# Splitting the experts' weights on Pool in layer 1 instead of layer 0 (a two-layer cross-attention and feed-forward kernel)

## The reference

```python
x = x + _L0_xattn_ref(_layernorm(x), ctx_768, ...)
x = x + _L0_ffn_ref(_layernorm(x), ...)        # int8-like fake quantisation, silu(gate) * up
x = x + _L1_xattn_ref(_layernorm(x), ctx_768, mask, ...)
x = x + _L1_ffn_ref(_layernorm(x), ...)        # 8 experts, all computed:

h = gelu(einsum('nd,edh->neh', xf, w1) + b1)   # w1: 8 x 128 x 256
y = einsum('neh,ehd->ned', h, w2) + b2         # w2: 8 x 256 x 128
out = (y * norm_g[:, None, None]).sum(axis=1)
```

## Time and profile before

| | us |
|---|---|
| median of 3 runs | 293.55 (293.08 to 295.0) |
| the profiled execution, its own time | 294.46 |
| the profiled execution, its span | 292.7 |
| PE busy | 265.0 (91%) |
| DVE busy | 205.5 (70%) |
| ACT busy | 203.7 (70%) |
| POOL busy | 101.6 (35%) |

### The profile page before, as it was taken

How to read it: one execution, slowest core, us unless ns; L and a number is a source line. 1 busy time by engine, 2 the same in 40 slices (tenths; PEclk the granted TensorE clock), 3 DMA queues, 4 the chain that set the end, 5 groups by cost and what they waited for, 6 DMA issues and landing times.

```text
span 292.7 us, 5757 instructions
## 1 busy us (share of the span) xinstructions
PE 265.0 (91%) x2075; PEld 189.3 (65%) x2075; DVE 205.5 (70%) x535; ACT 203.7 (70%) x303; POOL 101.6 (35%) x119
## 2 busy tenths in 40 slices
PE   8898989899998528888899999999999999999993
PEld 8776454655676217755545677776678578788872
DVE  3898776945996896799945886692548457745764
ACT  4735766188529837312677967898999996957991
POOL 3791996068950500120111000460202702107180
PEclk9999999999999995899999999999999999999999
DMA  7537000000000000000000000000000000000001
GB/s 232 164 85 212 1 2 3 0 2 0 2 1 2 0 0 0 2 0 1 2 3 2 0 2 0 2 0 3 0 36 3 0 0 2 0 37 2 0 1 72
DMA packets 4573, 6.45 MB, mean 22 GB/s; under 512 B 1181, under 2 KB 2898, under 8 KB 4546
## 3 DMA queue, kind: packets, MB, share of 16 engines
q1 hardware_dynamic: 3426, 3.47, 3.8%
q0 software_dynamic: 848, 2.35, 2.8%
q10 hardware_dynamic: 272, 0.27, 0.3%
HBM read 5.04 MB, written 1.05 MB: 21 GB/s over the span
## 4 chain that ended last, share of the span: by engine, by line
PE 53%; DVE 5%; ACT 2%; issue 2%; POOL 1%; DVEq 0%; POOLq 0%
PE ps L1107 6%; PE ps L1096 6%; PE ps L1109 5%; PE ps L1097 5%; PE ps L1098 5%; PE ps L1108 5%; PE ps L1006 3%; PE ps L988 2%; PE ps L947 2%; PE ps L968 1%; PE ps L1014 1%; PE ps L1042 1%; PE ps L1085 1%; DVE mxr L697 1%; ACT p L501 1%
## 5 line engine op out<-in xcount | busy, mean ns | idle before, releaser
L779 DVE TENSOR_TENSOR hhl<-hf,hhl 128x512 fp32r<-128x512 f32 x64 | 42.7, 689 | 26.7 <-ACT hf L571 24.0
L501 ACT ACTIVATE p<-ps 117x1024 f32<-117x1024 f32 (+1 forms) x48 | 46.2, 1021 | 15.1 <-PE ps L998 15.0
L697 DVE TENSOR_REDUCE mxr<-ps 128x8 f32<-128x616 f32 x64 | 47.6, 793 | 12.2 <-PE ps L978 12.0
L570 ACT ACTIVATE hhl<-ps,b 128x512 fp32r<-128x512 f32 x64 | 45.9, 717 | 10.4 <-PE ps L1109 6.0
L571 ACT ACTIVATE hf<-ps,b 128x512 f32<-128x512 f32 x64 | 46.0, 718 | 0.0
L888 PE MATMUL ps<-ones 128*128 128x128 f32 x230 | 36.8, 308 | 1.5 <-POOL ones L387 1.0
L888 PEld LDWEIGHTS ps<-ones 128*128 128x128 f32 x230 | 33.5, 219 | 6.5 <-issue 2.9
L344 POOL TENSOR_SCALAR veps<-mv 128x4 f32<-128x4 f32 x16 | 5.2, 327 | 81.8 <-DVE mv L627 81.6
L444 POOL TENSOR_TENSOR lq<-ebase,lg 128x32 f32<-128x32 f32 x4 | 22.3, 5587 | 19.0 <-DVE lg L818 18.9
L1107 PE MATMUL ps<-hhl,w2l 128*128 128x512 f32 x64 | 26.8, 419 | 0.0
L1096 PE MATMUL ps<-x1buf,w1l 128*128 128x512 f32 x64 | 26.4, 413 | 0.0
(11 more groups left out here) (188 smaller groups left out, 565.5 us busy)
## 6 DMA issues: line engine op xcount, KB each, us to landing
x<-in_x SPq DMA_DIRECT2D x4, 256.0 KB, 4.5
w1raw<-in_w POOLq DMA_DIRECT2D x1, 1024.0 KB, 6.3
w2raw<-in_w POOLq DMA_DIRECT2D x1, 1024.0 KB, 7.2
out<-xn SPq DMA_DIRECT2D x4, 256.0 KB, 2.1
ctxw<-in_ctxw SPq DMA_DIRECT2D x1, 280.0 KB, 5.1
kmo<-in_kmo POOLq DMA_DIRECT2D x1, 220.0 KB, 8.0
ctxw<-in_ctxw ACTq DMA_DIRECT2D x1, 192.5 KB, 3.5
wqo<-in_wqo SPq DMA_DIRECT2D x1, 192.0 KB, 5.6
```

The source lines that it names most:

```text
L501: act.activation(p[0:w, j, 2 * half:2 * half + 2, :], pair_of("key", u, j, half)[0:w], ACT.Exp, scale=SCALE).then_inc(q["p_ready"], 1)
L570: act.activation(hh[:, b % HR, :], bank_of("w1", 1, b), ACT.Gelu, bias=b1[:, b % NH:b % NH + 1])
L697: nc.vector.tensor_reduce(mxr[:, u % 2, j, 2 * half:2 * half + 2, :], heads[:, :, :, 0:M], AX.X, ALU.max).then_inc(q["tok_maxed"], 1)
L779: nc.vector.tensor_tensor(hl[:, b % HR, :], hf[:, b % HF, :], hh[:, b % HR, :].bitcast(F32), ALU.subtract).then_inc(q["h_lo"], 1)
```

## The change

The eight `w1split` and `w2split` jobs leave Pool's list of layer 0 and stand in its list of layer 1, among `down.b` and `wo.b`; the two branches that call `weights_split` move from the one loop to the other. No instruction is added or removed, and no other engine's list is changed. All line numbers above 76 become smaller by one to five.

```diff
     (1, "POOL"): """
-        down.0 down.1 down.2 down.3 wo.0 ga.0 wo.1 gb.0 ga.1 wo.2 gb.1 ga.2 wo.3 gb.2 ga.3 gb.3
+        down.0 down.1 w1split.0 w1split.1 down.2 w1split.2 down.3 w1split.3 w2split.0 w2split.1 wo.0 w2split.2 w2split.3 ga.0 wo.1 gb.0 ga.1 wo.2 gb.1 ga.2 wo.3 gb.2 ga.3 gb.3
     """,
...
-                if job == "w1split":
-                    weights_split(w1raw, w1h, w1l, b, "w1_in", "w1_split")
-                if job == "w2split":
-                    weights_split(w2raw, w2h, w2l, b, "w2_in", "w2_split")
                 if job == "hclear":
                     pool.wait_ge(q["vr_put"], 2 * B)
                     pool.wait_ge(q["v_set"], 2 * B)
...
                 if job == "wo":
                     rstd_of(3 * B + b)
+                if job == "w1split":
+                    weights_split(w1raw, w1h, w1l, b, "w1_in", "w1_split")
+                if job == "w2split":
+                    weights_split(w2raw, w2h, w2l, b, "w2_in", "w2_split")
```

More of the change, by code:

```diff
@@ L71 @@
     (0, "POOL"): """
-        lnstat.0 kmo.0 lnstat.1 mxset.0 lnstat.2 lnstat.3 bias.0 loads.0 loads.1 w2split.0 bias.1 kt.0 bias.2 bias.3 w2split.1 wo.0 w1split.0
-        w2split.2 w1split.1 w1split.2 wo.1 hclear.0 w2split.3 kmx.0 w1split.3 wo.2 wo.3
+        lnstat.0 kmo.0 lnstat.1 mxset.0 lnstat.2 lnstat.3 bias.0 loads.0 loads.1 bias.1 kt.0 bias.2 bias.3 wo.0 wo.1 hclear.0 kmx.0 wo.2 wo.3
     """,
```

## The result

The changed kernel takes 306.16 us (median of 4 runs, 304.37 to 306.41) against 294.26 us for the kernel before on the same chip (293.08 to 295.0). The ratio is 1.0395, with a 95% interval of 1.036 to 1.043: 11.9 us slower. The profiled execution has a span of 304.5 us, 11.8 more than before, so its trace can be laid beside the one of before.

The account below looks back on a forecast made before the run. PE was taken as the bound on the whole, never idle from 163 us, with the change's worth decided on DVE beside Pool. Terms -0.6 + 1.3 + 0.15 + 0.8 = +1.65 us on the 293.55 median gave 295.2 us, range 292.8 to 297.6.

Parts of the forecast that it names:

- Layer 0, -0.6: In layer 0, L685 no longer delayed beside a split, so DVE's add of wo.3 starts earlier: -0.6 us.
- the 0.6 us reach the end: Behind wo.3, DVE runs without a wait into what the feed-forward part waits for, so the 0.6 us gain carries through.
- e = 1.3 for all four places: At lnx.1, lnx.2, lnx.3 and layer 1's ln.0, DVE's four L639 become longer by e, taken as 1.3 us.
- the precedent at 74.16: Layer 0's four L639 beside a split took 2.44 us, 1.35 more than alone; used to size e.
- the highest bound, 2.0: Largest e at layer 1's norm steps, about 2.0 us, with DVE's first instruction going before the CAST.
- The strict alternation: Rival: in layer 1 each DVE instruction waits for one whole Pool instruction, e 2.0, sum +3.75, 297.3 us; chance 0.20.
- Slacks: Delay absorbed in layer 1: none at lnx.1, 1.17 us at lnx.2, 3.3 at lnx.3, 0.5 at ln.0.
- the cover holds for any e above: At lnx.3, 3.3 us of slack before PE's transposes, so no cost for any e considered.
- PE's clock: A clock change on PE from new pauses of about 1 us would make the forecast wrong; no size given.
- Absorbed delays: Rival: PE's pauses between 138 and 163 us swallow layer 1's delays except the first; 293.6 us, chance 0.13.
- Pool as the one that waits: Rival: in layer 1 DVE's four run in one go while Pool's CAST waits; only -0.6 left, 292.95 us, chance 0.17.

Follow-up runs that it names:

- e7_lnx3: e1_wait with the wait taken out for w1split.3, w2split.0 and w2split.1, directly behind down.3: 294.53 us, ratio 1.0015 to the kernel before.
- e2_fill: The changed kernel with 15 and 11 idle matmul pairs filling PE's two pauses, ahead of the transposes of lnx.1's batch and layer 1's ln.0: 301.58 us, ratio 1.0244.
- e5_one: The changed kernel with one split behind each of five norm steps, the last three splits after a wait for DVE's norm: 299.01 us, ratio 1.017.
- e1_wait: The changed kernel, but each split in layer 1 waits until DVE has applied the norm ahead of it: 293.4 us, ratio 0.9968 to the kernel before.
- e3_fine: The changed kernel with each split in eight Pool instructions of 128 columns, not two of 512: 295.73 us, ratio 1.0043.
- e8_act: The changed kernel with lnx.1 and layer 1's ln.0 applied by ACT, not DVE, Pool's order unchanged: 300.76 us, ratio 1.022.
- e6_ln0: e1_wait with the wait taken out for w2split.2 and w2split.3 alone, directly behind layer 1's wo.0: 298.1 us, ratio 1.0127.

## Why the prediction was wrong

It forecast 295.2 us, and 297.6 at most. By its own steps:

- **Layer 0, -0.6**: the mechanism was right, the size too large. L685 takes 0.14 us and `wo.3` follows PE's projection, as said, but only 0.46 us earlier: that projection itself starts 0.15 us later. DVE was 0.08 us late already before `ln.1`, and `ln.1` is longer; `on.3` did not wait for PE behind it, as the prediction had read, but followed DVE's own work at once. Of the 0.46 us 0.22 are left at `lnx.1`; before that DVE waits 0.18 us for PE ahead of the add of `down.1` (122.49). That "the 0.6 us reach the end" was wrong.
- **e = 1.3 for all four places**: this is the step that failed first. Measured: 2.97, 1.48, 3.02 and 2.98 us. The places and the mechanism were right, the term was mis-sized by more than a factor of two at three of them. There are two reasons. The first is how the precedent at 74.16 was read. The timeline of DVE before, in shorter windows, has its instructions nearly one by one:

```profile
74.16 0.35 DVE L639 TENSOR_SCALAR xn<-x,mv,rstd 128x128 f32<-128x128 f32 x1
74.44 1.69 DVE L639 TENSOR_SCALAR xn<-x,mv,rstd 128x128 f32<-128x128 f32 x2
75.79 0.81 DVE L639 TENSOR_SCALAR xn<-x,mv,rstd 128x128 f32<-128x128 f32 x2
```

The first ends at 74.51, 0.08 us behind the CAST (74.43), the second at 75.87, 0.08 us behind the subtraction (75.79), the fourth at 76.60, 0.09 us behind L375 (76.51). Only the third (75.79 to 76.13) passed freely, where the prediction counts two. So this group was held three times out of four already; it was short because it met the last 0.27 us of a CAST, one subtraction, and L375 (0.61 us). A price by precedent holds for the same Pool instructions, and behind `lnx.1`, `lnx.3` and `ln.0` the four instructions meet two CASTs and two subtractions, all in full. The second reason is the highest bound, 2.0, which let DVE's first instruction go ahead of the CAST. In the trace it is held as well, so that the four DVE instructions meet CAST, subtraction, CAST and subtraction, 0.61 + 1.26 + 0.61 + 1.26 = 3.74 us, and 3.97 us with the gaps. A group's time is then the sum of the first four Pool instructions, and the bound from above for e should have been this sum less the 1.1 us that the group takes alone, some 2.9 us.
- **The strict alternation** was there as a rival with 0.20, and it is what happened; but with the e of 2.0 its time was 297.3, and even so it would have missed.
- **Slacks**: at `lnx.2` 1.17 us of slack against an e of 1.48 gives 0.31, and PE's `max.1` went from 4.19 to 4.55 us late: right. At `ln.0` 2.98 less 0.5 gives 2.5; PE's transposes were 2.83 later, before the clock. At `lnx.3` the sentence "the cover holds for any e above" was wrong: it looked only at who waits for `lnx.3`'s result, not at what stands behind it on DVE, `on.0`, which had 1.8 us to spare; e7_lnx3 shows 0.8 us for it by its trace.
- **PE's clock** was named among what would make the forecast wrong and was given no price. This is the second step that failed, a term left at nothing. It cost 4.6 us (e2_fill), more than the whole predicted sum. The profile's page of the kernel before had it in view: the granted clock there is below full speed behind the long idle time ahead of layer 1 (the clock row of the slices, `95899` at its lowest). With an e of 3.0 the pause on PE was to be worked out as 0.57 + 3.0 us.
- **Absorbed delays, and Pool as the one that waits**: both fell; nothing was absorbed but the named slacks and the 1.8 us ahead of `on.0`, and Pool's CAST and subtraction kept their 0.61 and 1.26 us, though Pool does wait elsewhere (`veps` at 124.66).

With the right e the prediction's own sum would have been -0.6 + 3.0 + 0.3 + 0.8 + 2.5 = 6.0, and with 4.6 for the clock 10.6 of the 11.9 us. The direction was right and the place was right; the time fell outside the range because of these two terms.

## What to carry to other kernels

Before work is moved to an idle stretch of GpSimd, look at what VectorE runs there. Beside its `tensor_scalar` instructions from SBUF to SBUF the work was not free here, and right behind a norm step that releases such instructions each of them stood still for one whole GpSimd instruction. Here four of them took as long as the first four GpSimd instructions behind the step, with the gaps; the loss is this sum less their own time. Where fewer GpSimd instructions stood there, the rest ran at their own pace (`lnx.2`, e5_one). A wait on GpSimd took back all of the loss (e1_wait). Shorter instructions on the moved side took back most of it (e3_fine, 1.48 us in place of 4.09), but they made GpSimd's work longer and its next norm step late. Then follow the delay to TensorE: a pause there can be followed by a stretch at half clock that outlasts it. For slack, the next job on the delayed engine counts too, not only the consumer of the result.

## What the runs showed of the hardware

- In the hand-over between Pool and DVE beside the splits of layer 1, Pool went on each time after 0.07 to 0.08 us, and one DVE instruction got through in each of these gaps. At 74.16 in the kernel before, the gap behind the subtraction was 0.11 us (75.79 to 75.90) and one more DVE instruction passed, the third. L375 then took 0.61 us, where it takes 0.53 in the changed kernel. Whether the gap's length decides who goes first was not tested.
- Pool isn't always the winner: `veps` took 0.77 us in place of 0.23 behind a DVE instruction that was under way.
- PE's clock halved behind pauses of 3.6, 2.7 and 2.4 us (e8_act), but also behind one of 1.00 us (e3_fine, `lnx.1`). Pauses of 1.44 us (e8_act, `lnx.1`) and 1.54 us (e3_fine, `ln.0`) left it at 1.00, as one of 0.57 us did before. So the length of the last pause alone doesn't decide it. The stretch at half speed differed too: some 6.8 us in all behind each pause of the changed kernel, some 3.4 in e6_ln0 and in e3_fine. What exactly sets either stays open.
- Of the clock's 4.6 us, 3.1 lie behind the second pause. There PE is busy without a gap (2.00 of 2.00 us in the changed kernel's windows from 171 on, and 17.00 of 17.00 before), so every matmul that takes longer moves the end.
